# Quantised attention of one layer: scores matmuls over all 128 rows instead of 64, with the turned q kept twice and the other head's rows zero

## The chip, the cores and the metric

The kernel runs on one core of a Trainium2 chip. The metric is the device time of one execution in microseconds (us); several executions are timed and their median is given. One further execution is taken with the hardware profiler, and every row below is from that one. Its times count from the first instruction of the program.

## The reference

The program is a stack of eight layers over x of 8 examples x 128 tokens x 256 features: four cross-attentions and four feed-forward blocks by turns, each with a layer norm in front and a gated sum behind. In the profile they come one after another; here they are called A to H. The change touches only the fifth, E. What layer E computes is this:

```python
def _fq_sym(x, axis):
    s = jnp.maximum(jnp.max(jnp.abs(x), axis=axis, keepdims=True) / 127.0, 1e-08)
    return jnp.clip(jnp.round(x / s), -127.0, 127.0) * s      # forward value

q = (x @ Wq + bq).reshape(1, B * N, H, hd)                    # B*N = 1024, H = 16, hd = 16
kv = (cond @ Wkv + bkv).reshape(1, -1, 2, H, hd)
k, v = (kv[:, :, 0], kv[:, :, 1])
q = q * hd ** -0.5                                            # then heads first in q, k, v
q = _fq_sym(q, axis=-1)
k = _fq_sym(k, axis=-1)
v = _fq_sym(v, axis=2)
attn = softmax(einsum('bhqd,bhkd->bhqk', q, k))
attn = _fq_unsigned(attn, axis=-1)                            # 255 steps
out = einsum('bhqk,bhkd->bhqd', attn, v).reshape(B, N, C)
return out @ Wp + bp
```

(Shortened: the transposes are left out.) All 8 examples are one sequence here: 1024 queries against 1024 keys, for each of 16 heads.

## The kernel before, in words

**Numbers.** A rounded q is a whole number of at most 127 and fits bf16. A rounded k is a whole number times a step in fp32 and does not, so it is split into three bf16 parts (high, middle, low) that add up to it. The score of a head is then one matmul over 64 rows: 4 parts x 16 features. On the q side ("stack") the parts are three copies of q and a zero part; on the k side ("kstack") they are the three parts of k and a zero part. Two heads lie one above the other in 128 rows: the even head in rows 0 to 63, the odd one in rows 64 to 127. So the turned k, `E_kT`, has 8 pairs of heads x 1024 keys on 128 rows, and the turned q of an example, `E_[g]["qT"]`, 8 pairs x 128 queries.

**Units.** The layer works in units: one head of one example. Two examples (g = 0 and 1) make a step, and a step has 16 heads x 2 = 32 units; there are 4 steps, so 128 units. For a unit u:

- TensorE multiplies the scores (line 2282): two matmuls of 512 columns each, over the 64 rows of that head, into two PSUM banks.
- VectorE takes the maximum over 1024 keys (line 2451), and a small instruction makes the bias of it (line 2453).
- ScalarE takes the exponential of all 1024 with the sum beside it (line 2369).
- VectorE rounds it to bf16 whole numbers (line 2461).
- TensorE turns these in 8 pieces of 128 x 128 (line 2302), ScalarE copies the turned piece out of PSUM (line 2362), and TensorE weighs v with it: 8 matmuls of 16 columns (line 2320).

**Order.** Each engine has its own instruction stream, written out by slots. In slot n an engine does: the extra pieces of that slot, scores of unit n, weighing of unit n - 3, turning of unit n - 2 (TensorE); exponential of n - 2, copy of the turned piece of n - 3, extra pieces (ScalarE); reads, rounding of n - 2, extra pieces, maximum of n (VectorE). `E_pipeline` writes 8 slots, then a hardware loop of 3 iterations of 32 slots, then the 32 slots of the last step. The extra pieces prepare the next step while this one runs: layer norm of x (VectorE, slots 8 and 10), turning x (TensorE line 2257, slots 14 and 15), the projection of q (line 2263, slots 16 and 17), its rounding (up to slot 26), turning the q stack (line 2269, slots 30 and 31), and for the step that ends, the turn of the output (line 2338, slots 36 and 37) and its projection (line 2343, slots 38 and 39).

**The turned q.** `E_turn_stack` (line 2266) writes the turned q stack to PSUM bank 1 of its example, 128 rows x 1024 bf16. `E_q_T` (line 2352) is the copy to `qT` in SBUF, by ScalarE (line 2354). In the loop it first waits for the last scores of the running step that read `qT` (`E_scores`, in `extra` of `E_scalar`), and TensorE's turn of the unit before the next slot waits until bank 1 has been read (`E_qTs`, in `turn`). The scores of the next step wait for `E_qTs` as well.

**Ahead of the loops.** `E_before_...` make k, v and the first step's q for all examples: projections over the context (line 2071), rounding and splitting of k on VectorE and ScalarE, turns of the k stack (line 2080), and the copy to `E_kT` (line 2117). At its start `E_before_vector` (line 2138) clears the zero parts of the stacks (lines 2170 and 2171), then takes the first statistics of the norm.

**Space.** `spare` is 2048 words of SBUF at the start of a large tile that the profile calls "late". Layers A, D and G use it; layer E does not.

Of the kernel before, what the change touches and what calls it, by code (L numbers as in the profile page):

```python
# [20 lines left out]
BF16 = mybir.dt.bfloat16  # L21
# [4 lines left out]
P = 128  # L26
# [59 lines left out]
def program(nc, t, out, layers=8):  # L86

    with ExitStack() as ctx:
# [44 lines left out]
        def bank(g, n):  # L133
            return PS[:, 4 * g + n, :]
# [8 lines left out]
        spare, late = big[:, 0:2048], big[:, 2048:]  # L143

        def view(tile, at, *shape, dt=F32):

            n = 1
            for s in shape:
                n *= s
            words = n * (2 if dt in (BF16, F16, U16) else 4) // 4  # L150
            v = tile[:, at:at + words]
            if dt != F32:
                v = v.bitcast(dt)
            names = ["a", "b", "c", "d", "e"][:len(shape)]
            if len(shape) > 1:
                v = v.rearrange(f"p ({' '.join(names)}) -> p {' '.join(names)}", **dict(zip(names, shape)))
            return v, at + words
# [1372 lines left out]
        D_m, _ = view(spare, 0, 4, 2 * D)  # L1530
        D_turned_o, _ = view(spare, 0, KC, 512)
# [451 lines left out]
        HE, DE, TE = 16, 16, 8  # L1983
        ROWS = 64
# [8 lines left out]
        E_kT, _ = view(early, 0, TE, NB * P, dt=BF16)  # L1993
        E_vs = sb("E_vs", [P, 2, D])
        E_v, _ = view(work[:, 0, :], 4096, NB, D)
        E_vq, _ = view(work[:, 1, :], 5120, NB, D, dt=BF16)
        E_ = [{} for _ in range(G)]
        for g in range(G):
            w, n_ = work[:, g, :], 0
            E_[g]["stack"], n_ = view(w, n_, HE, 4, DE, dt=BF16)  # L2000
            E_[g]["qT"], n_ = view(w, n_, TE, P, dt=BF16)
            E_[g]["t"], n_ = view(w, n_, D)
            E_[g]["u"], n_ = view(w, n_, D)
            E_[g]["e"], n_ = view(w, n_, 1024)
            E_[g]["pb"], n_ = view(w, n_, 1024, dt=BF16)
            E_[g]["pT"], n_ = view(w, n_, NB, P, dt=BF16)
            E_[g]["oT"], n_ = view(w, n_, KC, P)
            k_, at_ = E_[g]["e"], 0
            E_[g]["kstack"], at_ = view(k_, at_, HE, 4, DE, dt=BF16)
            E_[g]["kt"], at_ = view(k_, at_, D)  # L2010
            E_[g]["ku"], at_ = view(k_, at_, D)
# [27 lines left out]
        E_qTs = flag("E_qTs")  # L2039
# [98 lines left out]
        def E_before_vector(dve, ch):  # L2138

            def rounded_k(b):  # L2140
                g = b % G
                e = E_[g]
                dve.wait_ge(E_kv.sem, E_kv.nth(0, b))
                if b >= G:
                    dve.wait_ge(E_ku.sem, E_ku.nth(0, b - G))
                nc.vector.tensor_tensor(E_v[:, b, :], bank(g, 0)[:, D:2 * D], E_bias[:, 2 * D:3 * D], ALU.add).then_inc(ctx_read[g], 1)
                read = nc.vector.tensor_tensor(e["kt"], bank(g, 0)[:, 0:D], E_bias[:, D:2 * D], ALU.add)
                read.then_inc(E_kvread.sem, 1)
                dve.wait_ge(E_kvread.sem, E_kvread.nth(0, b))
                s, r = root[:, g, 0:16], root[:, g, 16:32]  # L2150
                step_of(ch, e["kt"], s, 1e-8)
                ch.link(nc.vector.reciprocal(r, s))
                ch.link(nc.vector.tensor_tensor(heads16(e["kt"]), heads16(e["kt"]), over_d(r), ALU.mult))
                ch.link(nc.vector.tensor_scalar(e["kt"], e["kt"], MAGIC, MAGIC, ALU.add, ALU.subtract))
                nc.vector.tensor_tensor(heads16(e["kt"]), heads16(e["kt"]), over_d(s), ALU.mult).then_inc(E_kt.sem, 1)

            def less_high(b):
                e = E_[b % G]
                dve.wait_ge(E_khi.sem, E_khi.nth(0, b))
                if b >= G:  # L2160
                    dve.wait_ge(E_kstack.sem, E_kstack.nth(0, b - G))
                nc.vector.tensor_tensor(heads16(e["ku"]), heads16(e["kt"]), e["kstack"][:, :, 0, :], ALU.subtract).then_inc(E_ku.sem, 1)

            def less_middle(b):
                e = E_[b % G]
                dve.wait_ge(E_kmid.sem, E_kmid.nth(0, b))
                nc.vector.tensor_tensor(e["kstack"][:, :, 2, :], heads16(e["ku"]), e["kstack"][:, :, 1, :], ALU.subtract).then_inc(E_kstack.sem, 1)

            for g in range(G):
                ch.mark(nc.vector.memset(E_[g]["kstack"][:, :, 3, :], 0.0))  # L2170
                ch.mark(nc.vector.memset(E_[g]["stack"][:, :, 3, :], 0.0))
            ch.mark(nc.vector.memset(ones_b, 1.0))
            ch.mark(nc.vector.tensor_scalar(E_bias[:, 3 * D:4 * D], E_bias[:, 3 * D:4 * D], gates[:, 0, 2:3], None, ALU.mult))
            ch.restart()
            norm_stats(ch, 0)
            for b in range(NB + G):
                if b < NB:
                    rounded_k(b)
                if b == NB - 1:
                    nc.vector.tensor_reduce(E_vs[:, 1, :], E_v.rearrange("p b d -> p d b"), AX.X, ALU.max,  # L2180
                                            apply_absolute_value=True).then_inc(E_vmax.sem, 1)
                if b >= G:
                    less_middle(b - G)
                if 0 <= b - 1 < NB:
                    less_high(b - 1)
                if b == 0:
                    E_normed_x(dve, 0)
                if b == 2:
                    for g in range(G):
                        E_read_q(dve, 0, g)  # L2190
                if b in (3, 4):
                    E_quantised_q(dve, ch, 0, b - 3)
                    E_switch(ch, 0, b - 3)
# [79 lines left out]
        def E_tensor(pe):  # L2273
            def scores(ch, i, u):
                h, g = head_of(u), u % G
                if h == 0:
                    pe.wait_ge(E_qTs.sem, E_qTs.nth(i, g + G * (u // E_UNITS)))
                if u >= G:
                    pe.wait_ge(E_exp.sem, E_exp.nth(i, u - G))
                r = slice(ROWS * (h % 2), ROWS * (h % 2) + ROWS)  # L2280
                for n in range(2):
                    last = nc.tensor.matmul(bank(g, 2 + n), E_[g]["qT"][r, h // 2, :], E_kT[r, h // 2, n * 512:(n + 1) * 512],  # L2282
                                            start=True, stop=True)
                last.then_inc(E_scores.sem, 1)

# [65 lines left out]

        def E_q_T(act, i, g):
            act.wait_ge(E_qturned.sem, E_qturned.at(i, g))
            nc.scalar.copy(E_[g]["qT"].rearrange("p a b -> p (a b)"), bank(g, 1).bitcast(BF16)).then_inc(E_qTs.sem, 1)

        def E_scalar(act, ch):
            def p_T(ch, i, u):
# [157 lines left out]
        F_h, _ = view(work[:, 0, :], 0, 10, D)  # L2515
# [752 lines left out]
```

## Time and profile before

| what | value |
|---|---|
| median of 3 runs | 1687.25 us (1685.66 to 1689.84) |
| the profiled execution | 1686.88 us |
| its span, first to last instruction | 1685.1 us |
| granted TensorE clock, mean | 0.827 of full speed |
| layer E's loops in the span | from about 1085 to about 1413 us |

How to read the rows further down. A row of the timeline gives the start in us from the start of the span, the length in us, the engine (PE is a TensorE matmul, PEld its weight load, DVE VectorE, ACT ScalarE, POOL GpSimd), the line of the code, the operation, output and input by name, the shape, the number of instructions merged, and in brackets how long the engine idled before it and whom it waited for. In the shape of a matmul, 64\*128 means weights of 64 rows and 128 columns. A row of windows gives the stretch, its length, then for each engine the busy time and the count, then the granted clock (1.00 is 2.4 GHz, 0.50 is 1.2 GHz), then the share and rate of DMA. A row of a group gives the number of instructions, their busy time together and the mean length of one in ns, then the idle time before them. The ends of matmuls are modelled, so a block of TensorE can look some tenths longer than it is; starts are not.

### The profile page before, as it was taken

What the parts mean: (1) busy time and instruction counts of PE and PEld (TensorE: products, weight loads), DVE (VectorE), ACT (ScalarE), POOL (GpSimd) and SP (SyncE); (2) the same over time, 40 slices, a digit from 0 to 9 for tenths busy, and PEclk for the clock granted to TensorE, in tenths of its full rate; (3) what the DMA queues carried; (4) which work ended last, traced back from release to release, by engine and by line L of the source; (5) the groups of instructions that cost most, each with busy time, mean ns of one, the idle gap of its engine ahead of it and who ended that gap; (6) DMA issues with size and microseconds to landing.
All of it is one profiled execution on the core that took longest, in us unless ns stands there. A gap on an engine that the chain in (4) does not pass through costs nothing.

```text
span 1685.1 us, 26853 instructions
## 1 busy us (share of the span) xinstructions
PE 1363.3 (81%) x9111; PEld 957.5 (57%) x9124; DVE 1198.5 (71%) x2657; ACT 964.0 (57%) x2879; POOL 290.5 (17%) x369
## 2 busy tenths in 40 slices
PE   5775565379798898897689998498898998997898
PEld 4653444156566675675567776154454455775686
DVE  3786888669989889887443444888888887565353
ACT  2562676388677687785254561477777875232222
POOL 0000322234344353443000000000000000001000
PEclk7995787599999899999699999665757555996899
DMA  5302000100000000000600000000000001000000
GB/s 200 149 4 100 1 0 1 54 1 5 4 1 6 0 1 6 0 1 1 263 1 1 1 1 11 9 2 1 1 0 0 0 1 50 1 0 1 1 1 25
DMA packets 13583, 38.12 MB, mean 23 GB/s; under 512 B 2201, under 2 KB 8866, under 8 KB 10802
## 3 DMA queue, kind: packets, MB, share of 16 engines
q1 hardware_dynamic: 13490, 36.99, 5.8%
q8 instruction: 45, 0.74, 0.2%
q14 instruction: 48, 0.39, 0.1%
HBM read 35.94 MB, written 1.05 MB: 22 GB/s over the span
## 4 chain that ended last, share of the span: by engine, by line
PE 48%; DVE 33%; ACT 8%; issue 7%; POOL 1%; DVEq 0%; DMA 0%; ACTq 0%; POOLq 0%; another core or an unknown queue 0%
PE PS L2302 4%; PE PS L2282 4%; PE PS L2991 3%; DVE small L2451 3%; DVE work L1134 2%; PE PS L1375 2%; PE PS L1874 2%; DVE work L2461 2%; PE PS L690 2%; PE PS L1803 2%; PE PS L1367 2%; PE PS L1905 2%; DVE work L1161 2%; PE PS L1447 2%; PE PS L2661 1%
## 5 line engine op out<-in xcount | busy, mean ns | idle before, releaser
L2451 DVE TENSOR_REDUCE small<-PS 128x1 f32<-128x1024 f32 x128 | 156.0, 1219 | 18.6 <-PE PS L2282 14.7
L2369 ACT ACTIVATE work<-PS,small 128x1024 f32<-128x1024 f32 x128 | 155.0, 1211 | 9.8 <-DVE small L2453 8.6
L1250 POOL TENSOR_TENSOR small<-small,minus_half 128x4 f32<-128x4 f32 x96 | 107.0, 1115 | 267.4 <-ACT small L1290 266.9
L1375 PE MATMUL PS<-late 128*128 128x512 f16 x384 | 105.2, 406 | 57.5 <-DVE work L1177 34.3
L2302 PE MATMUL PS<-ident_b,work 128*128 128x128 bf16 x1024 | 121.3, 293 | 27.9 <-DVE work L2461 21.8
L2282 PE MATMUL PS<-early,work 64*128 64x512 bf16 x256 | 121.0, 571 | 5.4 <-ACT work L2369 3.3
L1340 ACT ACTIVATE work<-PS,small 128x128 f32<-128x128 f32 x256 | 90.5, 365 | 49.5 <-DVE small L1184 49.5
L212 POOL TENSOR_TENSOR rstd<-moments,eps 128x1 f32<-128x1 f32 x56 | 13.6, 242 | 597.4 <-DVE moments L192 597.2
L2362 ACT COPY work<-PS 128x512 f32<-128x512 f32 x128 | 75.0, 586 | 65.0 <-PE PS L2302 65.0
L2302 PEld LDWEIGHTS PS<-ident_b,work 128*128 128x128 bf16 x1024 | 91.4, 132 | 33.1 <-DVE work L2461 19.9
L1375 PEld LDWEIGHTS PS<-late 128*128 128x128 f16 x384 | 36.1, 101 | 111.2 <-DVE work L1177 46.1
L2320 PEld LDWEIGHTS PS<-work 128*128 128x128 bf16 x1024 | 36.9, 104 | 98.4 <-ACT work L2362 81.1
L2461 DVE TENSOR_SCALAR work<-work 128x1024 bf16<-128x1024 f32 x128 | 87.6, 684 | 7.3 <-ACT work L2369 5.1
L1306 ACT ACTIVATE work<-PS 128x128 f32<-128x128 f32 x256 | 67.3, 282 | 34.5 <-PE PS L1375 32.8
L1447 PEld LDWEIGHTS PS<-work 128*128 128x128 f32 x512 | 72.6, 213 | 12.0 <-ACT work L1333 7.7
L1447 PE MATMUL PS<-work 128*128 128x128 f32 x512 | 76.6, 298 | 3.2 <-ACT work L1333 3.0
L1261 POOL TENSOR_TENSOR work<-work 128x512 f16<-128x512 f32 x64 | 74.2, 1159 | 19.9 <-DVE work L1134 19.9
L1467 PE MATMUL PS<-work 128*128 128x256 f32 x256 | 66.6, 383 | 4.0 <-DVE work L1134 3.9
L1479 PE MATMUL PS<-late,work 128*128 128x256 f16 x480 | 64.5, 277 | 2.9 <-POOL work L1261 2.8
L1134 DVE TENSOR_TENSOR work<-work 128x512 f32<-128x512 bf16 (+1 forms) x96 | 57.9, 603 | 3.3
L1367 PE MATMUL PS<-late,ctxT 128*128 128x512 f32 x128 | 60.2, 592 | 0.0
L1479 PEld LDWEIGHTS PS<-late,work 128*128 128x128 f16 x480 | 47.7, 100 | 21.1 <-issue 9.1
(412 smaller groups left out, 3434.9 us busy)
## 6 DMA issues: line engine op xcount, KB each, us to landing
late<-in_C_proj SPq DMA_DIRECT2D x1, 4096.0 KB, 12.2
ctxT<-in_ctxT SPq DMA_DIRECT2D x24, 128.0 KB, 2.6
late<-in_C_q SPq DMA_DIRECT2D x1, 2048.0 KB, 8.2
late<-in_C_qx SPq DMA_DIRECT2D x1, 2048.0 KB, 12.6
late<-in_F_w SPq DMA_DIRECT2D x2, 1024.0 KB
late<-in_B_gate SPq DMA_DIRECT2D x1, 1024.0 KB, 8.6
late<-in_B_up SPq DMA_DIRECT2D x1, 1024.0 KB, 10.6
late<-in_B_down SPq DMA_DIRECT2D x1, 1024.0 KB, 12.4
```

The lines of the kernel that those rows point to most:

```text
L1134: return nc.vector.tensor_tensor(t, y, m, ALU.add)
L1250: return nc.gpsimd.tensor_tensor(rs, rs, minus_half[:, 0:4], ALU.pow)
L1340: last = nc.scalar.activation(C_[g]["p"][:, h, :], PS[:, SBANK, h * P:(h + 1) * P], ACT.Exp, scale=DC ** -0.5, bias=small[:, g, 8 + h:9 + ...
L1367: last = nc.tensor.matmul(PS[:, n, :], src(k), w[:, k, c0:c0 + 512], start=k == 0, stop=k == KC - 1)
L1375: last = nc.tensor.matmul(PS[:, n, :], src(k), w, start=k == 0 and part == 0, stop=k == KC - 1 and part == 1)
L1447: last = nc.tensor.matmul(PS[:, SBANK, h * P:(h + 1) * P], c["qT"][:, h, :], c["kT"][:, 2 * (r % 2) + h // 2, :], start=True, stop=True)
L1479: last = nc.tensor.matmul(PS[:, OUTBANK, g * D:(g + 1) * D], C_[g]["cat"][:, h, :], proj_part((4 * r + h) // 2, part)[:, h % 2, :], start= ...
L2282: last = nc.tensor.matmul(bank(g, 2 + n), E_[g]["qT"][r, h // 2, :], E_kT[r, h // 2, n * 512:(n + 1) * 512], start=True, stop=True)
L2302: last = nc.tensor.transpose(bank(g, 1).bitcast(BF16)[:, b * P:(b + 1) * P], E_[g]["pb"][:, b * P:(b + 1) * P], ident_b[:])
L2369: nc.scalar.activation(E_[g]["e"], banks(g, 2), ACT.Exp, scale=small[:, g, h:h + 1], bias=small[:, g, 48 + h:49 + h], accum_out=small[:, g ...
L2451: ch.link(nc.vector.tensor_reduce(small[:, g, 80:81], banks(g, 2), AX.X, ALU.max))
L2461: nc.vector.tensor_scalar(E_[g]["pb"], E_[g]["e"], MAGIC, MAGIC - 1.0, ALU.add, ALU.subtract).then_inc(E_pb.sem, 1)
```

## The change

It keeps the turned q of an example twice. `qT` now has the even heads in rows 0 to 63 and zeros below; the new `qT_odd`, in `spare`, has zeros in rows 0 to 63 and the odd heads below. The zeros are written once, by four memsets at the start of the layer. The copy out of PSUM becomes two copies of 64 rows each. The scores matmuls take all 128 rows: the k of both heads of a pair moves through, and the zeros of q remove the other head's share. Number and columns of the matmuls stay as they are.

```diff
@@ tiles of layer E
             E_[g]["stack"], n_ = view(w, n_, HE, 4, DE, dt=BF16)
             E_[g]["qT"], n_ = view(w, n_, TE, P, dt=BF16)
+            E_[g]["qT_odd"], _ = view(spare, 512 * g, TE, P, dt=BF16)
             E_[g]["t"], n_ = view(w, n_, D)
@@ E_before_vector
             for g in range(G):
                 ch.mark(nc.vector.memset(E_[g]["kstack"][:, :, 3, :], 0.0))
                 ch.mark(nc.vector.memset(E_[g]["stack"][:, :, 3, :], 0.0))
+                ch.mark(nc.vector.memset(E_[g]["qT"][ROWS:, :, :], 0.0))
+                ch.mark(nc.vector.memset(E_[g]["qT_odd"][0:ROWS, :, :], 0.0))
             ch.mark(nc.vector.memset(ones_b, 1.0))
@@ scores, in E_tensor
-                r = slice(ROWS * (h % 2), ROWS * (h % 2) + ROWS)
+                q_ = E_[g]["qT_odd" if h % 2 else "qT"]
                 for n in range(2):
-                    last = nc.tensor.matmul(bank(g, 2 + n), E_[g]["qT"][r, h // 2, :], E_kT[r, h // 2, n * 512:(n + 1) * 512],
+                    last = nc.tensor.matmul(bank(g, 2 + n), q_[:, h // 2, :], E_kT[:, h // 2, n * 512:(n + 1) * 512],
                                             start=True, stop=True)
@@ E_q_T
-            nc.scalar.copy(E_[g]["qT"].rearrange("p a b -> p (a b)"), bank(g, 1).bitcast(BF16)).then_inc(E_qTs.sem, 1)
+            for name, r in (("qT", slice(0, ROWS)), ("qT_odd", slice(ROWS, P))):
+                last = nc.scalar.copy(E_[g][name][r].rearrange("p a b -> p (a b)"), bank(g, 1).bitcast(BF16)[r])
+            last.then_inc(E_qTs.sem, 1)
```

## Rows read from the trace of the kernel before

**Rows 1.** The page, the 40 slices: granted clock of TensorE in tenths
```profile
PEclk7995787599999899999699999665757555996899
```

**Rows 2.** Windows of layer E: us, busy us (instructions) of each engine, clock, DMA
```profile
1085.30:1413.50 328.20, 292.75 (x2426) 159.44 (x2424) 284.25 (x471) 245.57 (x415) 16.73 (x31) 0.58 0.00 1
...
1376.00:1408.00 32.00, 32.00 (x271) 16.50 (x270) 30.36 (x46) 26.57 (x46) 0.00 (x0) 0.50 0.01 1
```

**Rows 3.** The chain of waits through layer E's loops, by line
```profile
by line: PE PS L2302 21.9%; PE PS L2282 20.0%; DVE small L2451 15.4%; DVE work L2461 9.3%; issue 7.0%; PE PS L2320 6.1%; PE PS L2263 2.8%; ACT work L2369 2.3%; PE PS L2343 2.3%; PE PS L2269 1.6%; ACT work L2354 1.0%; DVE stats L191 0.8%; PE
```

**Rows 4.** Timeline, a plain piece at clock 0.50: start us, us, engine, line
```profile
1386.28 0.38 PE L2320 MATMUL PS<-work 128*128 128x16 bf16 x8
...
1386.52 1.01 PE L2302 MATMUL PS<-ident_b,work 128*128 128x128 bf16 x8
...
1387.47 1.03 PE L2282 MATMUL PS<-early,work 64*128 64x512 bf16 x2
...
1388.43 0.38 PE L2320 MATMUL PS<-work 128*128 128x16 bf16 x8
```

**Rows 5.** Timeline, a plain piece at clock 1.00
```profile
1102.94 1.22 DVE L2451 TENSOR_REDUCE small<-PS 128x1 f32<-128x1024 f32 x1
...
1103.09 0.62 PE L2302 MATMUL PS<-ident_b,work 128*128 128x128 bf16 x8
...
1103.94 0.60 PE L2282 MATMUL PS<-early,work 64*128 64x512 bf16 x2 [0.23 <-ACT work L2369]
...
1104.93 1.22 DVE L2451 TENSOR_REDUCE small<-PS 128x1 f32<-128x1024 f32 x1
```

**Rows 6.** Windows of layers B, E, E and G, columns as in rows 2
```profile
200.00:220.00 20.00, 11.17 (x66) 7.99 (x66) 16.82 (x33) 17.36 (x34) 6.11 (x6) 0.83 0.00 0
...
1101.00:1106.00 5.00, 3.97 (x53) 2.42 (x54) 4.93 (x7) 4.91 (x10) 0.00 (x0) 1.00 0.00 0
...
1208.00:1216.00 8.00, 7.27 (x75) 4.65 (x73) 7.34 (x12) 6.05 (x12) 0.00 (x0) 0.93 0.00 0
...
1538.00:1547.80 9.80, 9.71 (x34) 7.29 (x34) 1.53 (x3) 3.47 (x10) 0.00 (x0) 0.50 0.00 0
```

**Rows 7.** Groups of instructions of layer G, 1538 to 1547.8 us
```profile
L2789 PE MATMUL PS<-work,ones 1*128 1x128 f32 x10 | 4.0, 497 | 0.0
```

**Rows 8.** Timeline of TensorE, turns with the q stack's turns behind them
```profile
1161.56 1.01 PE L2302 MATMUL PS<-ident_b,work 128*128 128x128 bf16 x8
...
1162.37 0.85 PE L2269 MATMUL PS<-ident_b,work 128*128 128x128 bf16 x6
```

**Rows 9.** Timeline of VectorE, the maxima that begin and end the iterations
```profile
1110.29 1.22 DVE L2451 TENSOR_REDUCE small<-PS 128x1 f32<-128x1024 f32 x1
...
1358.62 1.22 DVE L2451 TENSOR_REDUCE small<-PS 128x1 f32<-128x1024 f32 x1
...
1407.86 1.22 DVE L2451 TENSOR_REDUCE small<-PS 128x1 f32<-128x1024 f32 x1
```

**Rows 10.** Timeline of VectorE, maxima around the projection of q, two iterations
```profile
1126.43 1.23 DVE L2451 TENSOR_REDUCE small<-PS 128x1 f32<-128x1024 f32 x1 [0.50 <-PE PS L2282]
...
1134.41 1.22 DVE L2451 TENSOR_REDUCE small<-PS 128x1 f32<-128x1024 f32 x1
...
1209.88 1.23 DVE L2451 TENSOR_REDUCE small<-PS 128x1 f32<-128x1024 f32 x1
...
1215.22 1.22 DVE L2451 TENSOR_REDUCE small<-PS 128x1 f32<-128x1024 f32 x1
```

**Rows 11.** Timeline, the boundary between two steps
```profile
1164.50 1.01 ACT L2354 COPY work<-PS 128x1024 bf16<-128x1024 bf16 x1 [1.30 <-PE PS L2282]
...
1165.66 1.01 PE L2302 MATMUL PS<-ident_b,work 128*128 128x128 bf16 x8 [0.95 <-ACT work L2354]
```

**Rows 12.** Groups of instructions of VectorE, memsets
```profile
L278 DVE MEMSET late<- 128x1024 f32 x2 | 1.8, 912 | 5.1 <-DMA X<-in_x 5.0 <-issue 0.2
...
L2170 DVE MEMSET work<- 128x128 uint32 x2 | 0.3, 165 | 0.0
```
## The prediction, made before the kernel was run

> **What bounds the kernel now.** I began with the page's 40 slices, for the granted clock along the span. Slices 25 to 33, where layer E (the changed one) runs, are granted 0.5 to 0.7 of full speed, where the layers beside it have 0.9 and more [rows 1]. Layer E's loops take 328.2 us, a fifth of the program; in them TensorE is busy for 292.75 us and VectorE for 284.25 us, and the mean clock is 0.58 [rows 2]. So two engines are near their limit, and one of them runs at 1.2 of its 2.4 GHz most of the time. The chain of waits through that stretch names TensorE's turns (line 2302) and scores (line 2282) for 21.9% and 20.0%, VectorE's maximum (line 2451) and rounding (line 2461) for 15.4% and 9.3% [rows 3]: the end is set now by the one, now by the other.
>
> Next the timeline of a plain piece, with nothing in it but the units (one head of one example each). From 1376 to 1408 us the clock is 0.50 and TensorE is busy for 32.00 of 32.00 us [rows 2]. One unit there goes from one weighing to the next in 1388.43 - 1386.28 = 2.15 us [rows 4]. At the full clock the same unit takes 1104.93 - 1102.94 = 1.99 us from maximum to maximum [rows 5], and VectorE is busy for 4.93 of 5.00 us [rows 6]. So at 1.2 GHz TensorE bounds a plain unit, and at 2.4 GHz VectorE does, only 0.16 us lower. That caps the gain.
>
> **Does the change move the clock?** The columns streamed, the matmuls and their number stay; only the rows of a scores matmul go from 64 to 128. So the question is whether rows count. Layer B, whose matmuls all use 128 rows, is granted 0.83 with TensorE busy for 11.17 of 20.00 us. Layer G, where 4.0 of 9.80 us are matmuls over one row, is granted 0.50 with TensorE busy for 9.71 of 9.80 us, and layer E's plain piece the same with 32.00 of 32.00 [rows 2, 6, 7]. Busy time does not order these three; busy time over full rows does. In layer E itself the clock rises to 0.93 in the piece from 1208 to 1216 us [rows 6], right behind the fp32 turns of x and during the projection of q, both over 128 rows. I take it that full rows in the scores lift the plain pieces to 2.4 GHz. The Trainium skill says otherwise (TensorE: Matmul & The Clock Gate, Part 1): the clock goes by how busy the engine has been, and no row count comes into it; its Part 4 adds that turns count for less. By that rule the change leaves the clock where it is (second case below). The trace speaks against the first half: a fully busy engine at 0.50.
>
> **The switch between row shapes.** Eight turns followed by another block of 128-row turns start 1162.37 - 1161.56 = 0.81 us apart [rows 8]; eight turns followed by the 64-row scores 1387.47 - 1386.52 = 0.95 us [rows 4]. Two scores matmuls of 512 columns need 2 x 512 / 1.2 GHz = 0.85 us; the weighing behind them starts 1388.43 - 1387.47 = 0.96 us after them. That is 0.14 + 0.11 = 0.25 us in every unit, lost around the 64-row shape. With 128 rows all shapes are alike, and I take the whole of it away: TensorE would need 2.15 - 0.25 = 1.90 us for a plain unit even at 1.2 GHz, under VectorE's 1.99. The Trainium skill agrees (TensorEngine Tiling (Array Packing), Key Properties): a change of tiling mode drains the engine.
>
> **The sum.** Three loop iterations of 32 units run from 1110.29 to 1358.62 us, 82.8 us each, and 23 plain units to 1407.86 [rows 9].
> - Plain units: about 14 in each iteration and 23 behind them, 65 x 0.16 = 10.4 us.
> - The two units that carry the projection of q take 1134.41 - 1126.43 = 7.98 us at 1.2 GHz and 1215.22 - 1209.88 = 5.34 us at 2.4 [rows 10]. Two iterations of three are at the low clock: 2 x 2.64 = 5.3 us.
> - The two units before the step boundary run one after another: scores, ScalarE's copy of the turned q, turns. The scores go from 1.03 to 0.60 us, the turns from 1.01 to 0.62 [rows 4, 5], the turns of the q stack, of the same shape as the latter, by 0.4 too: 6 units x 1.2 = 7.2 us. No row shows these at 2.4 GHz; between nothing and 1.2 us each, I take the upper end, since TensorE is named in each wait there [rows 11].
> - Some eight further units per iteration wait for TensorE (turns of x and of the output, first units of a step), 0.25 us each: 6.0 us. An estimate: half of the 0.43 us that the scores alone gain.
> - The switches gone in units that wait for TensorE at 2.4 GHz too: half of 0.25 us in some 20 units, 2.5 us.
>
> Gross 31.4 us. The clock will not hold everywhere: where a step begins, TensorE does less, since it waits for the others. I take off 15%, an estimate: 26.7 us.
>
> Against it stands ScalarE's second copy. The copy of the turned q waits for the last scores of the step, and the turns and ScalarE's own next exponential wait for it (the turns with 0.95 us idle) [rows 11]. It takes 1.01 us for 1024 elements in each row. No row shows it over 64 rows: it lies between half of that and the whole. The elements in each row stay 1024, so I take the whole: 6 in the loops x 1.01 = 6.1 us on the path. The two copies ahead of the loops lie on ScalarE, which idles there behind VectorE: nothing, or 2 us if that cover is gone. Four new memsets of 1024 bf16 = 512 words stand on VectorE in front of the layer's first statistics. Such a memset of 1024 words takes 0.91 us, one of 128 words 0.165 us [rows 12], so by their line 0.48 us each, 1.9 us in all, and VectorE leads there: all of it counts. (If the idle behind them hid it, nothing.)
>
> Sum: -26.7 + 6.1 + 1.9 = -18.7 us. The profiled execution took 1686.9 us (span 1685.1, 1.8 around it), 0.4 below the median of the runs, so 1686.9 - 18.7 = 1668.2, told as 1668. A change of 0.3%, 5.1 us, is about what a measurement can tell from none.
>
> **Other ways it could go.**
> - *Clock and switches both move* (the forecast), 0.77. Its own range: the boundary term may be nothing (+6), the copies half (-3), the clock loss none or double (-5, +5): 1657 to 1679.
> - *The clock stays, the switches go*, 0.13. This is what the Trainium skill's rule on the clock gives. For it: turns are nearly half of the columns and I can't see apart whether they count; against it: the three stretches above. Plain units still fall to 1.99, as TensorE needs 1.90: 10.4 us. Some 30 units that wait for TensorE gain 0.2 us: 6 us. Less 8.0 for copies and memsets: 1686.9 - 8.4 = 1678.5.
> - *Slower: neither moves, and the copy at the boundary is what is left*, 0.10. Price 6 x 1.01 + 1.9 = 8.0 us: 1695. It decides as soon as the gain on TensorE is under 8 us. For it: the waits in [rows 11] show that nothing covers the copy. Against it: the 0.25 us around the 64-row shape would have to be a cost of the scores as such. If ScalarE's two copies ahead of the loops count as well, 1697.
> - That TensorE would take longer for 128 rows than for 64, I leave out: the two scores matmuls already start the weighing 0.96 us later, of which their 1024 columns at 1.2 GHz are 0.85.
>
> **How the numbers follow.** The likeliest case gives 1668. The range 1656 to 1681 takes in nearly all of it and most of the second case, and leaves out the slower one and the tails, about 2 in 10. Faster by over 0.3% (under 1682): nearly all of the first case and four fifths of the second, 0.87. Within 0.3%: 0.05. Slower: 0.08.
>
> **What would show it.** In the profile after: the clock of slices 25 to 33 at 0.8 to 1.0; in the plain piece 1.99 us from maximum to maximum, VectorE without idle time and TensorE's busy time well under the stretch; scores blocks of 0.60 us; no extra gap between turns and scores; two copies of 1.01 us for each example at a boundary, with the turns waiting some 2 us for them; four memsets of about 0.48 us. The clock at 0.50 with units of 1.99 us would say second case; units of 2.15 us the third. Wrong would be: full clock, yet more than 80 us for an iteration, which would mean that the boundary chain, not TensorE's rate, holds the time.

## The result, and the profile after

The kernel with the change took 1672.14 us (median of 6 runs, 1667.73 to 1674.7), the kernel before 1688.54 us beside it (6 runs, 1685.66 to 1689.84): a ratio of 0.9903 (95% interval 0.9885 to 0.992), 16.4 us less. Forecast were 1668 us and a range of 1656 to 1681. The profiled execution has a span of 1671.4 us against 1685.1.

The page's granted clock in 40 slices, and two of its groups. A group reads: busy us, mean ns of one, then the idle time before them.

```profile
PEclk7995777599999899999679999769898898996999
...
L2456 DVE TENSOR_REDUCE small<-PS 128x1 f32<-128x1024 f32 x128 | 155.6, 1216 | 4.8 <-PE PS L2285 3.9
...
L2305 PE MATMUL PS<-ident_b,work 128*128 128x128 bf16 x1024 | 90.4, 239 | 66.0 <-DVE work L2466 52.3
```

The same two groups before the change:

```profile
L2451 DVE TENSOR_REDUCE small<-PS 128x1 f32<-128x1024 f32 x128 | 156.0, 1219 | 18.6 <-PE PS L2282 14.7
...
L2302 PE MATMUL PS<-ident_b,work 128*128 128x128 bf16 x1024 | 121.3, 293 | 27.9 <-DVE work L2461 21.8
```

Slices 25 to 33 (counted from 0) rose from between 0.5 and 0.7 [rows 1] to between 0.6 and 0.9, and the slices ahead of them are much as they were. VectorE's 128 maxima have 4.8 us of idle time before them in all, where they had 18.6, mostly for TensorE's scores. TensorE's turns wait 66.0 us, where they waited 27.9, mostly for VectorE's rounding: the roles have changed.

Two windows, with the columns of [rows 2]: all of layer E's loops, and a plain piece.

```profile
1087.00:1401.00 314.00, 218.57 (x2411) 137.15 (x2455) 280.54 (x475) 260.51 (x430) 17.38 (x32) 0.86 0.00 1
1350.00:1390.00 40.00, 29.46 (x355) 16.66 (x363) 39.30 (x62) 37.67 (x61) 0.00 (x0) 1.00 0.01 1
```

TensorE is busy for 218.57 us, where it was 292.75, at a mean clock of 0.86 instead of 0.58. In the plain piece VectorE is busy for 39.30 of 40.00 us. The chain of waits through the loops says the same:

```profile
by line: DVE small L2456 36.9%; DVE work L2466 21.5%; issue 12.4%; PE PS L2305 5.0%; ACT work L2374 2.6%; ACT late L2358 1.9%; PE PS L2346 1.8%; PE PS L2266 1.8%; PE PS L2285 1.6%; DVE small L2458 1.3%; ACT early L2118 0.9%; DVE stats L191 
```

The maximum and the rounding, both VectorE's, make 58.4% of it. The turns and the scores, 21.9% and 20.0% before [rows 3], are down to 5.0% and 1.6%. A new name is ScalarE's second copy, "ACT late L2358", at 1.9%.

The timeline of a plain unit at the full clock: start us, length us, engine and line.

```profile
1371.94 1.22 DVE L2456 TENSOR_REDUCE small<-PS 128x1 f32<-128x1024 f32 x1
1372.08 0.62 PE L2305 MATMUL PS<-ident_b,work 128*128 128x128 bf16 x8 [0.32 <-DVE work L2466]
...
1372.81 0.60 PE L2285 MATMUL PS<-early,work 128*128 128x512 bf16 x2
...
1373.38 0.36 PE L2323 MATMUL PS<-work 128*128 128x16 bf16 x8
...
1373.92 1.22 DVE L2456 TENSOR_REDUCE small<-PS 128x1 f32<-128x1024 f32 x1
```

Maximum to maximum is 1.98 us, and the scores block takes 0.60 us as it did over 64 rows [rows 5]. But the clock is not at the full rate everywhere. A window and the timeline of a patch at the lower level:

```profile
1199.50:1203.50 4.00, 3.11 (x31) 1.91 (x31) 3.93 (x8) 3.06 (x7) 1.35 (x2) 0.59 0.00 0
```
```profile
1199.49 1.22 DVE L2456 TENSOR_REDUCE small<-PS 128x1 f32<-128x1024 f32 x1
...
1201.47 1.22 DVE L2456 TENSOR_REDUCE small<-PS 128x1 f32<-128x1024 f32 x1
...
1201.61 1.03 PE L2305 MATMUL PS<-ident_b,work 128*128 128x128 bf16 x8 [0.47 <-DVE work L2466]
...
1203.45 1.22 DVE L2456 TENSOR_REDUCE small<-PS 128x1 f32<-128x1024 f32 x1
```

The turns take 1.03 us, which is the 1.2 GHz length, and still the units are 1.98 us apart, with TensorE idle for 0.47 us ahead of the turns. So in this patch VectorE, not TensorE, sets the time of a plain unit over full rows at the lower level too. The evidence is thin: such patches hold only a few plain units each; the first of the two intervals is 1.98 us in the kernel before as well; the second was 2.18 us there, but the clock is at 1.2 GHz for only about two thirds of it here. In the first iteration, where the clock was at 1.2 GHz for all of that same unit, it took 2.07 us. The experiments below come back to it.

The step boundary, which stood at one copy before [rows 11]:

```profile
1164.87 1.01 ACT L2358 COPY work<-PS 64x1024 bf16<-64x1024 bf16 x1 [0.36 <-PE PS L2285]
...
1165.89 1.01 ACT L2358 COPY late<-PS 64x1024 bf16<-64x1024 bf16 x1
...
1167.04 0.61 PE L2305 MATMUL PS<-ident_b,work 128*128 128x128 bf16 x8 [2.09 <-ACT late L2358]
...
1171.28 1.01 PE L2305 MATMUL PS<-ident_b,work 128*128 128x128 bf16 x8 [2.08 <-ACT late L2358]
```

Half the rows did not make the copy shorter: 1.01 us each, as for 128 rows. TensorE waits 2.09 us and 2.08 us for the second of them. VectorE's new memsets, from its groups between 1040 and 1050 us:

```profile
L2173 DVE MEMSET work<- 64x512 uint32 x2 | 1.0, 485 | 0.3 <-issue 0.3
L2174 DVE MEMSET late<- 64x512 uint32 x2 | 1.0, 485 | 0.3 <-issue 0.3
```

485 ns each and 0.16 us of issue gap with each.

Where the time went, worked out from the starts of the first memset, the first statistics and the maxima in the profiled executions (us). A unit's time here runs from its maximum to the next one. "Boundary" is the last three units of a step, once in each of three iterations, "q projection" the two units that carry it, "others" the rest of the 96. The kernel before was profiled once, so how well its stretches repeat is not known.

```
stretch                         before    after     difference
layers A to D, unchanged        1039.36   1042.98    +3.6
memsets of layer E                 1.01      3.60    +2.6
to the first maximum              45.86     46.83    +1.0
first eight units                 24.06     23.92    -0.1
iterations: q projection          21.30     16.17    -5.1
            boundary              32.02     32.08    +0.1
            others               195.01    182.58   -12.4
last 23 plain units               49.24     45.58    -3.7
rest                             277.24    277.62    +0.4
span                            1685.1    1671.4    -13.7
```

Of the +3.6 us in unchanged layers nothing is the change's doing. All profiled executions of this study, with the same code there, have 1037.4 to 1044.8 us for it. Without it the profiled executions differ by 17.4 us.

### The profile page after: what moved, and what is told of

Its sections match the earlier page's. It is cut to its first block, busy times and chain, and to the rows that moved or that the text cites. A ratio compares the mean times of both kernels' runs of the same rounds, so it can differ in the third digit from the quotient of the medians.

```text
span 1671.4 us, 26822 instructions
## 1 busy us (share of the span) xinstructions
PE 1293.7 (77%) x9068; PEld 938.0 (56%) x9124; DVE 1195.9 (72%) x2661; ACT 975.7 (58%) x2887; POOL 290.9 (17%) x369
## 4 chain that ended last, share of the span: by engine, by line
PE 40%; DVE 40%; ACT 9%; issue 8%; POOL 1%; DVEq 0%; DMA 0%; ACTq 0%; POOLq 0%; another core or an unknown queue 0%
DVE small L2456 7%; DVE work L2466 4%; PE PS L2996 3%; PE PS L1375 2%; DVE work L1134 2%; PE PS L1874 2%; PE PS L1803 2%; PE PS L690 2%; PE PS L1367 2%; PE PS L1905 2%; PE PS L1447 2%; DVE work L1161 1%; DVE small L1183 1%; DVE work L1199 1%; PE PS L2666 1%
## 5 line engine op out<-in xcount | busy, mean ns | idle before, releaser
L2305 PE MATMUL PS<-ident_b,work 128*128 128x128 bf16 x1024 | 90.4, 239 | 66.0 <-DVE work L2466 52.3
L2305 PEld LDWEIGHTS PS<-ident_b,work 128*128 128x128 bf16 x1024 | 66.2, 107 | 77.2 <-DVE work L2466 51.8
L2996 PE MATMUL PS<-work,late 128*128 128x256 f32 x256 | 56.0, 379 | 0.7 <-ACT work L2961 0.7
## 6 DMA issues: line engine op xcount, KB each, us to landing
late<-in_C_qx SPq DMA_DIRECT2D x1, 2048.0 KB, 12.4
```

The source lines that it names most:

```text
L2305: last = nc.tensor.transpose(bank(g, 1).bitcast(BF16)[:, b * P:(b + 1) * P], E_[g]["pb"][:, b * P:(b + 1) * P], ident_b[:])
L2996: last = nc.tensor.matmul(PS[:, bank_ + c % 2, n * D:(n + 1) * D], wH[name][:, k, at:at + P], H_rT[:, k, :], start=k == 0, stop=k == KC - 1)
```

## The experiments

Ten runs, each with the kernel before on the same chip. Medians and ratios are of timed runs, the stretches of profiled executions. **Theory A** is the forecast's: full rows raise the clock, and the switches between row shapes go. Its rivals are that only one of the two matters, or that busy time alone sets the clock.

**1. Half the rows back, all else kept (rows64).** The copies, the zeros and the memsets stay, only the scores read 64 rows again:

```diff
+                    r = slice(ROWS * (h % 2), ROWS * (h % 2) + ROWS)
-  nc.tensor.matmul(bank(g, 2 + n), q_[:, h // 2, :], E_kT[:, h // 2, ...
+  nc.tensor.matmul(bank(g, 2 + n), q_[r, h // 2, :], E_kT[r, h // 2, ...
```

> The changed kernel with one thing undone: the scores matmuls take 64 rows again, of qT for even heads and of qT_odd for odd heads. Memsets, both copies and the number of columns stay as changed, so only the rows of a scores matmul differ. My theory (full rows lift the clock and do away with the switch between shapes): clock in the plain piece back to 0.50, plain units back to 2.15 us, and the costs of the change alone are left, 6.1 us for copies and 2.6 for memsets: about 8 to 9 us slower than before, 1696 to 1698 us. Rival (the gain comes from the layout, for instance from the second tile): most of the 16 us gain stays, about 1672. Second rival (copies and memsets are hidden): the same as before, 1688.

Measured: 1701.42 us (1692.97 to 1703.11), ratio 1.009 (1.0073 to 1.0107). The page's clock, a window of plain units, and the boundary's timeline:

```profile
PEclk8995787599999999999799999675757555996899
```
```profile
1370.00:1400.00 30.00, 30.00 (x254) 15.54 (x253) 28.48 (x43) 24.95 (x42) 0.00 (x0) 0.50 0.01 1
```
```profile
1164.58 1.01 ACT L2359 COPY late<-PS 64x1024 bf16<-64x1024 bf16 x1
1165.73 1.01 PE L2306 MATMUL PS<-ident_b,work 128*128 128x128 bf16 x8 [1.96 <-ACT late L2359]
```

TensorE is again busy for all of a window, at 0.50, in units of 2.15 us. So the rows carry the whole gain, and what the change adds is a loss by itself. That loss can be read: the boundary units take 38.45 us against 32.02, so 6.44 us for six second copies, 1.07 each, beside the 2.6 us of memsets. Against this kernel, full rows take 6.37 us from the boundary. One thing stays open: 8 to 9 us of loss had been expected, and the medians differ by 15.5 (1701.42 and 1685.9). The profiled execution, 1692.97 us, is the shortest of five, and where the other 8 us of the median lie no trace shows. Two hints are on record: its layers A to D, 1037.4 us, are the shortest of all profiled executions, and its mean granted clock is 0.833, against 0.817 to 0.826 in the other four.

**2. Full-row work added to the kernel before (filler).** Ten matmuls per pair of units, over 128 rows, whose result nobody reads; the scores stay at 64 rows:

```diff
+                if g == 0:
+                    for _ in range(10):
+                        nc.tensor.matmul(bank(0, 0)[:, D:2 * D], ident_b[:], E_vq[:, 0, :], ...)
                 for b in range(NB):
```

> The kernel before with its 64-row scores, and ten extra matmuls of 128 rows x 256 bf16 columns ahead of the weighing of each unit of example 0, into the free half of its output bank; their result is not used. TensorE does more work here, not less. If the clock follows the work over full rows: the stretch of plain units is granted 1.00, and although TensorE has 1.07 us more to do in every second unit at 2.4 GHz, plain units fall from 2.15 to about 1.99 us; a total of 1670 to 1685 us. If the clock goes by busy time alone (TensorE was already busy all the time) or by something particular to the scores: it stays at 0.50, the extra columns need 2.1 us per pair, a pair takes 6.4 us in place of 4.3, and the total is about 120 us longer, near 1800.

Measured: 1690.77 us (1685.6 to 1694.92), ratio 1.0018 (1.0003 to 1.0032). A window and a timeline of plain units:

```profile
1365.00:1400.00 35.00, 30.84 (x374) 20.36 (x373) 32.59 (x50) 28.36 (x49) 0.00 (x0) 1.00 0.01 2
```
```profile
1372.71 0.60 PE L2282 MATMUL PS<-early,work 64*128 64x512 bf16 x2 [0.38 <-ACT work L2372]
1373.25 1.27 PE L2321 MATMUL PS<-work,ident_b 128*128 128x256 bf16 x10
1374.35 0.35 PE L2323 MATMUL PS<-work 128*128 128x16 bf16 x8
1374.56 0.61 PE L2302 MATMUL PS<-ident_b,work 128*128 128x128 bf16 x8
```

The clock went to 1.00 with more work and less busy time than before (30.84 of 35.00 us against 32.00 of 32.00 [rows 2]). That fits full rows and speaks against busy time; it also shows that the changes of row shape, which are all still there, do not by themselves keep the clock down. The time did not follow (1670 to 1685 us had been expected): the filler sits between scores and weighing, delays the next unit's turns, and makes pairs of 1.99 + 2.33 us. The place was badly chosen, so the kernel says what moves the clock, not what the clock is worth. Run 9 mends that for the plain units.

**3. A quarter of the heads with full rows (quarter),** as rows64, but every fourth head reads all 128:

```diff
+                    r = slice(0, P) if h % 4 == 0 else slice(ROWS * (h % 2), ROWS * (h % 2) + ROWS)
```

> The changed kernel with 128-row scores only for every fourth head and 64 rows for the others. Theory of the switches (0.25 us per unit lost around the 64-row shape, apart from the clock): the clock stays at 0.50 in the plain piece, since three quarters of the scores have half the rows; the units with 128 rows have turns and scores 0.81 us apart instead of 0.95 and the weighing 0.85 us behind the scores instead of 0.96, so that the plain piece averages 2.09 to 2.12 us, and the total is about 3 us under that of rows64. Rival (the whole gain is the clock's): no gap shrinks, 2.15 us in every plain unit. Second rival (any full-row scores are enough for the clock): 1.00 in the plain piece and 1.99 us.

Measured: 1696.54 us (1690.63 to 1697.78), ratio 1.0049 (1.0032 to 1.0066). None of the three expected cases came: the clock stayed at neither level, with 0.67 over the plain piece from 1366 to 1400 us, and the last 23 plain units average 2.05 us. So rows shift the share of time at each level. It also puts both shapes side by side at 1.2 GHz, in TensorE's timeline:

```profile
1394.89 1.01 PE L2306 MATMUL PS<-ident_b,work 128*128 128x128 bf16 x8
1395.84 1.03 PE L2286 MATMUL PS<-early,late 64*128 64x512 bf16 x2
1396.80 0.38 PE L2324 MATMUL PS<-work 128*128 128x16 bf16 x8
1397.04 1.01 PE L2306 MATMUL PS<-ident_b,work 128*128 128x128 bf16 x8
1397.84 1.06 PE L2286 MATMUL PS<-early,work 128*128 128x512 bf16 x2
1398.73 0.38 PE L2324 MATMUL PS<-work 128*128 128x16 bf16 x8
```

Eight turns to 64-row scores: 0.95 us; to 128-row scores: 0.80. Scores to weighing: 0.96 and 0.89 here. Over the whole trace, where nothing else is waited for, the last turn to the first scores matmul is 247 ns into the 64-row shape and 107 ns into the 128-row one at 1.2 GHz, and the last scores matmul to the first weighing 563 and 427 ns. So a switch costs 140 ns on the way in and 136 ns on the way out; at 2.4 GHz 96 ns (152 against 56) and 92 ns (308 against 216). The two 64-row matmuls themselves start 400 ns apart at 1.2 GHz, those over 128 rows 426, which gives 26 ns back: 0.25 us in all, the forecast's figure measured in one trace. In the Trainium skill (TensorEngine Tiling (Array Packing), Key Properties) changing the tiling mode needs a drain. The trace agrees, and has the price.

**4. The same kernel once more (before_clear).** The label misnames it: it is the kernel of run 3, executed once more on another chip.

> The kernel with 128-row scores in every fourth head again, for one more profile: at a clock of 0.50, turns and 128-row scores start 0.80 us apart and turns and 64-row scores 0.95; where the clock stands at 0.50 for a whole group of eight units, the two with 128 rows take 1.98 to 2.06 us and the others 2.15.

Measured: 1691.57 us in a single run. Its last 23 plain units took 47.32 us and those of run 3 47.19, both between 49.24 (before) and 45.58 (after); its boundary 36.83 against 36.80. There the in-between state repeats. It doesn't everywhere: the first iteration took 85.68 us against 82.34, the other two the same to 0.05 us. As expected, turns and 64-row scores start 0.95 us apart at 1.2 GHz, and the full-row units of the last plain piece take 1.98 to 2.06 us; turns and full-row scores, expected 0.80 us apart, are 0.89 us apart there.

**5. The changed kernel once more (again),** as a measure of repetition.

> The changed kernel once more, beside the others on one chip: 1668 to 1675 us, plain units of 1.98 us at a clock of 1.00.

Measured: 1673.83 us (1668.64 to 1675.57), ratio 0.9911 (0.9888 to 0.9934). Iterations of 77.52, 77.04 and 76.35 us against 77.47, 77.03 and 76.32: each repeats to 0.05 us. Layers A to D took 1044.78 us against 1042.98, so the difference between these two executions comes from there.

**6. The zeros written by GpSimd (pool_clear),** behind its adding of the bias, with TensorE's first scores waiting for them:

```diff
-                ch.mark(nc.vector.memset(E_[g]["qT"][ROWS:, :, :], 0.0))
-                ch.mark(nc.vector.memset(E_[g]["qT_odd"][0:ROWS, :, :], 0.0))
+                nc.gpsimd.memset(E_[g]["qT"][ROWS:, :, :], 0.0).then_inc(E_cleared, 1)
...
+                nc.gpsimd.memset(E_[g]["qT_odd"][0:ROWS, :, :], 0.0).then_inc(E_cleared, 1)
```

> The changed kernel with the four memsets moved from VectorE to GpSimd, behind its norm and bias work at the start of the layer; TensorE waits for them before its first scores. Theory (the memsets stand on VectorE's path): the stretch from the first memset to the first statistics falls from 3.60 us back to 1.01, and the total by 2.6 us, about 1669 to 1670 (0.9888 of before). Rival (they were hidden behind the projection of k and v): no gain in the total. A change of that size is close to what five rounds can tell, so the stretch itself decides.

Measured: 1667.79 us (1663.99 to 1672.04), ratio 0.9894 (0.9875 to 0.9914). GpSimd's groups:

```profile
L2219 POOL MEMSET late<- 64x1024 bf16 x2 | 1.9, 960 | 0.1
```

The stretch of VectorE's memsets is back at 1.01 us from 3.60, and nothing behind it grew by more than 0.5 us. So all 2.6 us had lain on the path. The two intervals overlap with those of the change as made; the trace resolves this, the timing alone doesn't.

**7. One copy each for ScalarE and VectorE (split_copy),** on top of run 6:

```diff
-            for name, r in (("qT", slice(0, ROWS)), ("qT_odd", slice(ROWS, P))):
-                last = nc.scalar.copy(E_[g][name][r]..., bank(g, 1).bitcast(BF16)[r])
-            last.then_inc(E_qTs.sem, 1)
+            nc.scalar.copy(E_[g]["qT"][0:ROWS]..., ...[0:ROWS]).then_inc(E_qTs.sem, 1)
+        def E_q_T_odd(dve, i, g):
+            dve.wait_ge(E_qturned.sem, E_qturned.at(i, g))
+            nc.vector.tensor_copy(E_[g]["qT_odd"][ROWS:]..., ...[ROWS:]).then_inc(E_qTo.sem, 1)
```

> As pool_clear, and the odd heads' copy of the turned q goes to VectorE, beside ScalarE's copy of the even heads; both wait for the last scores of the step as before. Theory (the second copy stands in series at the boundary): the two boundary units, 3.9 + 4.7 us now, lose one copy each, about 2.0 us per boundary and 6 us in three, so about 1663 to 1665 us. Rival (VectorE is the bound, so a copy of about 1 us on it costs as much as it saves): about the time of pool_clear.

Measured: 1664.76 us (1660.21 to 1665.33), ratio 0.9869 (0.9851 to 0.9888). The boundary's timeline, and VectorE's group of copies:

```profile
1159.66 1.01 ACT L2369 COPY work<-PS 64x1024 bf16<-64x1024 bf16 x1 [0.37 <-PE PS L2295]
1160.01 0.69 DVE L2373 COPY late<-PS 64x1024 bf16<-64x1024 bf16 x1
...
1160.92 0.61 PE L2317 MATMUL PS<-ident_b,work 128*128 128x128 bf16 x8 [1.19 <-DVE late L2373]
```
```profile
L2373 DVE COPY late<-PS 64x1024 bf16<-64x1024 bf16 x6 | 4.2, 694 | 0.2
```

The two copies overlap, TensorE waits 1.19 us instead of 2.09, and the boundary units take 24.89 us instead of 31.94 in run 6: 7.1 us for six copies taken from ScalarE. The second copy was fully on the path. Part of this is paid back elsewhere: the two such copies ahead of the loops now stand on VectorE, and its way from the first statistics to the first maximum grows by 1.3 us (46.51 to 47.80). The medians are 3.0 us apart, and the two ratios' intervals overlap, so here too the trace decides.

**8. Filler on top of that (split_filler):** four full-row matmuls per pair, where TensorE waits for the transposed weights anyway.

```diff
+                if g == 0 and h:
+                    for _ in range(4):
+                        nc.tensor.matmul(bank(0, 0)[:, D:2 * D], ident_b[:], E_vq[:, 0, :], ...)
                 pe.wait_ge(E_pT.sem, E_pT.nth(i, u))
```

> As split_copy, with four extra matmuls of 128 rows x 256 bf16 columns ahead of the weighing of each unit of example 0 that is not a first head (result not used). It asks what the rest of the low clock in layer E costs. If low clock in the pieces around the boundaries still costs time: the mean clock of the loops rises from 0.86 towards 1.00 and 2 to 5 us go, 1659 to 1662. If VectorE and the chain at the boundary set these pieces: the clock rises and the time stays or grows by what the filler delays the turns, 1664 to 1670.

Measured: 1661.34 us (1657.36 to 1663.68), ratio 0.9853 (0.9833 to 0.9872). The windows of the loops, first split_copy, then split_filler:

```profile
1087.00:1401.00 314.00, 224.95 (x2421) 141.94 (x2465) 289.11 (x511) 252.36 (x425) 18.84 (x36) 0.86 0.02 7
```
```profile
1087.00:1401.00 314.00, 235.42 (x2674) 163.28 (x2715) 292.04 (x524) 252.42 (x427) 18.84 (x36) 0.94 0.02 7
```

The clock rose from 0.86 to 0.94, and units that begin at the lower level fell from 27 to 8 of 96. The 96 units took 223.61 us and 223.52. So with full rows the clock that is still missing costs nothing that these traces show. The median, 1661.34 us, falls into the range of the other case, but the intervals of the two ratios overlap, and the 2.1 us between the two profiled spans lie in layers A to D, which differ by 2.3 us.

**9. The clock without full rows (clock_alone):** the kernel before with that same filler, in that same place; one copy, no zeros.

> The kernel before with its 64-row scores, one copy and no new memsets, and four extra matmuls of 128 rows x 256 bf16 columns for each unit of example 0 that is not a first head, placed ahead of the wait for the turned piece, where TensorE would idle at the full clock (result not used). It keeps the clock up and leaves the switches in. If the clock alone carries the gain on TensorE: plain units of 1.98 to 2.0 us at a clock of 1.00, the last 23 units in 45.6 to 46.5 us in place of 49.24, iterations of about 77 us, and without copies and memsets a total of 1665 to 1672. If the switches between shapes are needed for it: plain units stay at 2.05 us or more although the clock is 1.00, and the total is 1675 to 1685.

Measured: 1677.42 us (1677.22 to 1678.92), ratio 0.9951 (0.9934 to 0.9967). The page's clock, a window, and the timeline of a plain unit:

```profile
PEclk8895777599999999999799999776787799996899
```
```profile
1350.00:1390.00 40.00, 34.14 (x400) 20.70 (x398) 38.68 (x61) 35.44 (x58) 0.00 (x0) 1.00 0.01 1
```
```profile
1371.64 1.22 DVE L2454 TENSOR_REDUCE small<-PS 128x1 f32<-128x1024 f32 x1
...
1372.51 0.60 PE L2282 MATMUL PS<-early,work 64*128 64x512 bf16 x2
1373.04 0.61 PE L2318 MATMUL PS<-work,ident_b 128*128 128x256 bf16 x4
...
1373.62 1.22 DVE L2454 TENSOR_REDUCE small<-PS 128x1 f32<-128x1024 f32 x1
```

Where the clock holds, 64-row scores give the same 1.98 us: the last 23 units took 45.57 us, after the change 45.58. But inside the iterations it doesn't hold: 47 of 96 units begin at the lower level (before 79, after 24), and the iterations took 84.02, 78.07 and 84.35 us against 83.91, 79.95 and 84.46. This kernel gains in the plain units and in one iteration, and nothing in the other two. There the filler also costs: at the lower level its four matmuls keep the weighing back by 0.82 us (1154.83 to 1155.65 us), and the unit that begins at 1154.93 us takes 3.00 us, where it took 2.15 before. So neither expected case came whole: plain units behave as if the clock alone did it, the total lies in the other range, and for the iterations this run is no clean measure of the clock.

**10. A second set of buffers (two_sets),** on top of run 7: the turned q of the next step goes into another pair, so that no copy waits for the last scores of this one. The set lies in space that the values used before, and the loop over steps is written out.

```diff
+            E_[g]["qT1"], _ = view(work[:, 0, :], 4096 + 1024 * g, TE, P, dt=BF16)
+            E_[g]["qT_odd1"], _ = view(work[:, 0, :], 4608 + 1024 * g, TE, P, dt=BF16)
-                    act.wait_ge(E_scores.sem, E_scores.nth(i, E_UNITS - G + g))
-                    dve.wait_ge(E_scores.sem, E_scores.nth(i, E_UNITS - G + g))
```

> As split_copy, with a second set of qT and qT_odd, used by turns from step to step, and the loop over the steps written out, so that the copies of the next q no longer wait for the last scores of the running step. Theory (the boundary is expensive because scores, copy and turns follow one another): the boundary units fall from about 7 us a pair to about 5, and the total is 6 us under split_copy or more, about 1656 to 1659. Rival (the copies take the same time from engines that are full anyway): within 2 us of split_copy.

Measured: 1658.68 us (1652.31 to 1661.4), ratio 0.9831 (0.9808 to 0.9853), the fastest of all. The median is 6.1 us under run 7, as expected, but not for the reason given: the boundary's time stayed where it was (24.95 us against 24.89) instead of falling by 2 us a pair, so the buffer was not what it waited for. The rest of the 96 units shrank from 198.72 to 196.67 us; whether by the buffers or by the loop that is written out, no run tells. Against run 7 the intervals overlap; against the change as made, and against the kernel before, they don't.

## Why the prediction was right, and where a term was off

The likeliest case happened: clock up, switches gone, VectorE the bound of a plain unit. Full rows together were forecast at 26.7 us; from rows64 to after the traces give 27.0 (23.2 in the 96 units, 3.8 in the last 23), and the medians of rows64 and of the run again, on one chip, 27.6. By its own steps, each compared from before to after unless said otherwise:

- **What bounds the kernel:** right. A unit at 1.98 us with VectorE busy for 39.30 of 40.00 us is what [rows 5, 6] had shown.
- **Rows move the clock:** right, and shown from both sides. With the same columns streamed, rows64 stays at 0.50 where full rows have 1.00, and full-row filler lifts the kernel before. The rule that the Trainium skill gives (TensorE: Matmul & The Clock Gate, Part 1), by busy time alone, fails here: the window with 30.00 of 30.00 us busy is the one at 0.50. But the forecast's own argument did not bear its conclusion. It said that busy time over full rows orders its three stretches. From its rows, that is 11.17 of 20.00 us in layer B (0.56) and 9.71 - 4.0 = 5.7 of 9.80 us in layer G (0.58), and the one was granted 0.83, the other 0.50. The conclusion stands on rows64 and filler, not on those rows.
- **The switches:** 0.25 us forecast, 0.25 us measured at 1.2 GHz.
- **Plain units:** the last 23 gained 3.66 us, forecast 23 x 0.16 = 3.7, or 3.1 with the 15% off.
- **Projection of q:** 5.1 us, forecast 5.3, or 4.5 with the 15% off.
- **Boundary:** 7.2 us less 15%, so 6.1 us, forecast off it, and 6.1 us on it for the copies. Measured were 6.37 off (rows64 to after) and 6.44 on (before to rows64). Net, nothing. Taking the copy over 64 rows at its full 1.01 us was right. The gain lies in the first two of the three units, 3.06 and 3.32 us; the third, which runs over ScalarE's copies and exponential and VectorE's rounding, took 4.71 us with either row shape.
- **Others:** plain units of the iterations 42 x 0.16 = 6.7 us, with 6.0 and 2.5 for those that wait, 15.2 us, or 12.9 with the 15% off. Measured 12.4, but not made up like that, so the total is in part luck. Of the 81 units in it 44 did not change, 21 gained 0.11 to 0.20 us each, 3.4 us together, and 16 gained 0.29 to 1.31 us each, 9.0 us together. About half as many units as counted had 0.16 us to give. (The 0.25 us a unit behind the 6.0 was called half of 0.43, which is 0.22.)
- **Memsets:** mis-sized. 1.9 us forecast, 2.6 measured. The step took 0.48 us from the line through two durations and left out the 0.16 us of issue gap with each.
- **Not foreseen:** 1.0 us between the memsets and the first maximum, where VectorE waits 1.10 us for a projection of TensorE's at 1.2 GHz (at 1055.54 us), and the drift of layers A to D. The two second copies ahead of the loops, put at nothing or 2 us, cost 0.3 us at most (46.20 us in rows64 against 45.86).
- **The range of the first case:** its own terms give 1668 - 8 = 1660 at the low end, not the 1657 that it states.

The sum was -18.7 us. The profiled executions say -17.4 without the drift, the medians -16.4. The memsets' 0.7 us and the 1.0 ahead of the first maximum cover the missing 1.3 us. Of the signs, the clock fell short: 0.8 to 1.0 was named for slices 25 to 33, and two of the nine have 0.7 and 0.6.

One reason was weaker than it read. The forecast took off 15% because the clock wouldn't hold, and it had itself worked out that a plain unit over full rows needs only 1.90 us of TensorE at 1.2 GHz. The second is what counts. 24 of the 96 units begin at the lower clock, and raising it further brought nothing that the traces show (run 8). For plain units either effect would nearly do: the clock alone gives 1.98 us (run 9), and full rows at 1.2 GHz gave 1.98 to 2.16 us in the few units there are, where the same units over 64 rows took 2.15 to 2.57. Inside the iterations full rows also hold the clock where the filler did not, but the filler had a cost of its own there. How the 23.2 us that full rows take from the 96 units (rows64 to after) divide between the two over all units stays open: no run keeps full rows at 1.2 GHz throughout.

The slower rival, with neither moving, came true in rows64: 1693.0 us for the profiled execution, where 1695 was worked out; the median, 1701.4 us, is above it.

## What to carry to other kernels

A scores block over half of the rows took as long here as one over all of them (0.60 us at 2.4 GHz), and it cost twice beside that: it let the clock fall, and each change of row shape stalled TensorE for 0.09 to 0.14 us. How much a faster TensorE is worth depends on the next engine: only 37 of the 81 units outside the boundary and the projection of q got any shorter. Filling the other rows with zeros removes both, at the price of whoever has to place the operand twice. Put that second copy on another engine than the first, and the zeros on an engine with nothing due: here the traces give 7.1 us (of which 1.3 is lost again ahead of the loops) and 2.6 us for these two, beside the 17.4 us of the change itself.

## What the hardware showed that was not expected

- **ScalarE and VectorE on half the rows.** 1024 bf16 from PSUM take ScalarE 1.01 us over 64 rows as over 128; VectorE takes 0.69 us over 64.
- **Clock and rows.** The same matmuls and columns gave 0.50 or 1.00 by rows alone, even where half of the rows are zeros. With a quarter of the heads at full rows the mean was 0.67 in the plain piece.
- **The switch scales less than the clock.** 140 ns at 1.2 GHz and 96 ns at 2.4: at twice the clock less than a third of it is gone.
- **Unchanged layers drift.** A to D took 1037.4 to 1044.8 us over twelve profiled executions of the same code, while each iteration of layer E repeated to 0.05 us in the changed kernel. With the clock in between (runs 3 and 4) one of three iterations differed by 3.3 us. The windows from 600 to 800 us, before and after:

```profile
600.00:800.00 200.00, 176.70 (x1069) 129.76 (x1068) 168.86 (x374) 146.60 (x652) 81.40 (x76) 0.97 0.01 2
```
```profile
600.00:800.00 200.00, 177.91 (x1063) 130.05 (x1062) 168.66 (x373) 147.53 (x654) 81.47 (x76) 0.95 0.01 2
```

The same work, the same lines, and a granted clock that differs by 0.02. The profile doesn't tell what decides it. A gain of 3 us in one layer is better read from that layer's own stretch than from the whole, and from more than one profiled execution where the clock changes level inside it.
